# A grouped convolution on TensorE cut into four 32-row pieces, and the start of the program put into another order

## The reference

```python
def _L0_cond_ref(x, c, weight, c_weight, bias):      # grouped convolution, N, C, L = 32, 32, 512
    out = lax.conv_general_dilated(x, weight, window_strides=(1,), padding=[(4, 4)],
                                   dimension_numbers=('NCH', 'OIH', 'NCH'), feature_group_count=4)   # 9 taps
    return out + einsum('nd,od->no', c, c_weight)[:, :, None] + bias[None, :, None]
...
    q, k, v = x @ Wq.T, x @ Wk.T, x @ Wv.T           # 32 query heads, 8 key heads, of 128; RMS norm of q and k
...
    x = x + attention(conv(x, cond_128, ...), Wq, Wk, Wv, Wo, ...)      # ALiBi, causal, 32 keys a sample
    x = x + ffn(cond2(x, cond_128, ...), int4 weights ...)              # cond2: an 8-expert gate of two GELU layers
```

## Time and profile before

| | |
|---|---|
| Time, median of 3 runs | 699.32 us (698.92 to 699.69) |
| Profiled execution | 699.47 us, of which the span of the trace is 697.6 us |
| PE busy | 682.2 us, 98% of the span |
| DVE, ACT, POOL busy | 551.8, 422.9, 468.1 us |
| Clock of PE, mean granted | 0.996 |

### The profile page before, as it was taken

One profiled execution on the slowest core, in us unless ns is written; L12 is line 12 of the kernel. 1 busy time (PEld: TensorE's weight loads), 2 busy tenths in 40 slices (PEclk: granted clock), 3 DMA queues, 4 the chain that ended last, 5 costly groups with the idle time before them and its releaser, 6 DMA issues.

```text
span 697.6 us, 14570 instructions
## 1 busy us (share of the span) xinstructions
PE 682.2 (98%) x5070; PEld 402.7 (58%) x5070; DVE 551.8 (79%) x834; ACT 422.9 (61%) x1269; POOL 468.1 (67%) x380
## 2 busy tenths in 40 slices
PE   9999999999999999999999999999899999999996
PEld 8766555656656566565665656656535555555554
DVE  4978878878869778787886977777666888888887
ACT  0478483844746557384474656637556777767773
POOL 0468874973876595497388659558337778878885
PEclk9999999999999999999999999999999999999999
DMA  7520364685387378357528627544100000010001
GB/s 244 191 87 2 136 153 109 151 214 101 83 189 160 100 152 215 91 131 226 112 68 224 129 89 157 125 100 85 9 1 1 0 1 1 1 46 16 1 0 61
DMA packets 92752, 69.20 MB, mean 99 GB/s; under 512 B 74752, under 2 KB 75296, under 8 KB 90528
## 3 DMA queue, kind: packets, MB, share of 16 engines
q1 hardware_dynamic: 92560, 68.34, 39.1%
q10 hardware_dynamic: 144, 0.26, 0.1%
HBM read 51.68 MB, written 2.21 MB: 77 GB/s over the span
## 4 chain that ended last, share of the span: by engine, by line
PE 83%; POOL 6%; DVE 4%; issue 4%; ACT 2%; DMA 1%; SPq 0%; DVEq 0%; POOLq 0%; ACTq 0%
PE bank L612 20%; PE bank L613 19%; PE bank L614 19%; PE bank L972 3%; PE bank L973 3%; PE bank L941 3%; PE bank L942 3%; PE bank L664 2%; PE bank L959 2%; PE bank L960 2%; POOL wqlo L1984 2%; PE bank L801 1%; PE bank L759 1%; PE bank L786 1%; PE bank L774 1%
## 5 line engine op out<-in xcount | busy, mean ns | idle before, releaser
L612 PE MATMUL bank<-wohi,oThi 128*128 128x512 f16 x256 | 97.1, 379 | 2.2 <-DVE oTlo L1666 2.1
L612 PE MATMUL bank<-wqhi,cThi 128*128 128x512 f16 x256 | 97.0, 379 | 0.8 <-POOL wqlo L1984 0.6
L613 PE MATMUL bank<-wolo,oThi 128*128 128x512 f16 x256 | 97.0, 379 | 0.0
L614 PE MATMUL bank<-wohi,oTlo 128*128 128x512 f16 x256 | 97.0, 379 | 0.0
L614 PE MATMUL bank<-wqhi,cTlo 128*128 128x512 f16 x256 | 97.0, 379 | 0.0
L613 PE MATMUL bank<-wqlo,cThi 128*128 128x512 f16 x256 | 97.0, 379 | 0.0
L1129 ACT ACTIVATE qraw<-bank 128x512 f32<-128x512 f32 x64 | 37.8, 591 | 78.4 <-PE bank L614 77.6
L1674 DVE SCALAR_TENSOR_TENSOR x<-bank,ysc,x 128x512 f32<-128x512 f32 x64 | 47.8, 748 | 45.0 <-PE bank L614 44.8
L2032 POOL TENSOR_TENSOR qinv<-qms,neghalf 128x8 f32<-128x8 f32 x28 | 52.6, 1879 | 39.0 <-ACT qms L1148 39.0
L1140 ACT ACTIVATE qsq<-qraw 128x128 f32<-128x128 f32 x256 | 75.4, 299 | 1.7
L1994 POOL TENSOR_TENSOR wolo<-wor,wohi 128x512 f16<-128x512 f32 x32 | 40.3, 1278 | 49.6 <-ACT wohi L1109 49.6
(11 more groups left out here) (217 smaller groups left out, 1853.8 us busy)
## 6 DMA issues: line engine op xcount, KB each, us to landing
wqr<-in_wq SPq DMA_DIRECT2D x8, 1024.0 KB, 7.4
wor<-in_wo SPq DMA_DIRECT2D x8, 1024.0 KB, 6.0
raw<-in_gu_w SPq DMA_DIRECT2D x28, 256.0 KB, 3.1
zeros<-in_gu_z SPq DMA_DIRECT2D x28, 256.0 KB, 4.5
wkvr<-in_wkv SPq DMA_DIRECT2D x8, 512.0 KB, 7.2
srow<-in_up_s SPq DMA_DIRECT2D x14, 256.0 KB, 5.2
raw<-in_dn_w SPq DMA_DIRECT2D x14, 256.0 KB, 2.7
zeros<-in_dn_z SPq DMA_DIRECT2D x14, 256.0 KB, 3.7
```

Source lines behind the costliest of these rows:

```text
L612: mm(o, ahi, bhi, start=start and k == 0, stop=False)
L613: mm(o, ahi, blo, start=False, stop=False)
L614: last = mm(o, alo, bhi, start=False, stop=stop and k == n - 1)
```

## The change

Each 128-row matmul of the convolution becomes four of 32 rows, one for each channel group: group `g` has its channels and phases in partitions 32g to 32g + 31 (the host lays `xT` and `cwr` out so), its moving weights are 32 by 32 with no zeros, and it writes its own bank: `bank[4 * half + g]` for all four quads of a half. `cwf`, `mask` and their load are gone. So `conv_out` is called for a half and a group, after the half's last quad; and the maximum over `cf` is one reduction over a half.

The first query weights aren't scaled in place: ACT writes `wqhi` from `wqr` with the scale, DVE writes `wqlo` with it. Unit 0's `wqlo` no longer runs on POOL.

The order changes: the gate's whole chain stands between quads 3 and 4; quads 6 and 7 behind the first projection; `maxima_rows(2)` and `maxima_all(2)` later, between the last key and value tiles; the table load for Exp and the Exp before `conv_high(0)` on ACT; the reductions over `wqr`, `wkvr` and `cf` behind all of half 0's `conv_out` and the gate on DVE.

```diff
-            def conv(q, samples=range(BQ)):
+            def conv(q):
+                half, t = divmod(q, HQ)
                 pe.wait_ge(arrived[q], 16)
-                if q >= 2:
-                    pe.wait_ge(d_cf, q - 1)
-                out4 = PA[q % 2][:, :].rearrange("p (c b s) -> p c b s", c=PH, b=BQ)
-                for b in samples:
+                if q == 0:
+                    pe.wait_ge(l_conv, 16)
+                elif q == HQ:
+                    pe.wait_ge(d_ctxb, 2)
+                    pe.wait_ge(d_lg, 1)
+                for b in range(BQ):
                     for j in range(SHIFTS):
-                        last = mm(out4[:, :, b, :], xT[:, BQ * q + b, j:j + P], cwf[:, j, :, :, :],
-                                  start=j == 0, stop=j == SHIFTS - 1)
-                if b == BQ - 1:
-                    last.then_inc(t_conv, 1)
+                        for g in range(NGRP):
+                            rows = slice(PH * CG * g, PH * CG * g + PH * CG)
+                            out4 = bank[HQ * half + g][:, :].rearrange("p (c t b o) -> p c t b o", c=PH, t=HQ, b=BQ)
+                            last = mm(out4[:, :, t, b, :], xT[rows, BQ * q + b, j:j + P], cwr[rows, j, :, :],
+                                      start=j == 0, stop=j == SHIFTS - 1)
+                            if t == HQ - 1 and b == BQ - 1 and j == SHIFTS - 1:
+                                last.then_inc(t_conv, 1)
 
             pe.wait_ge(d_ones, 1)
             for _ in range(8):
                 mm(PC[3][:, 0:P], ones[:, :], ones[:, :], start=True, stop=True)
-            pe.wait_ge(d_cwf, 1)
             conv(0)
+            conv(1)
             context()
-            conv(1)
             conv(2)
+            conv(3)
             gate_layer1()
-            conv(3)
             gate_layer2()
+            gate_logits()
+            gate_spread()
             conv(4)
-            gate_logits()
-            conv(5, range(1))
+            conv(5)
             maxima_rows(1)
-            conv(5, range(1, 3))
             maxima_all(1)
-            conv(5, range(3, BQ))
-            conv(6)
-            gate_spread()
-            conv(7)
 
 
             def project_q(u, half, kv, t):
...
                 if half == 0 and t == 0 and not (isinstance(u, int) and u == 0):
-                    pe.wait_ge(p_wq, KC * kv + KC)
+                    pe.wait_ge(p_wq, KC * kv)
...
-                if not half:
-                    pe.wait_ge(d_cf, NQ - 1 if t == 0 else NQ)
                 project_q(u, half, 0, t)
 
             first_project_q(0, 0, 0)
+            conv(6)
+            conv(7)
             first_project_q(0, 0, 1)
             first_project_q(0, 0, 2)
+            first_project_q(0, 0, 3)
+            project_kv(0, 0, 0, (0,))
             maxima_rows(2)
-            first_project_q(0, 0, 3)
+            project_kv(0, 0, 0, (1,), (2,))
             maxima_all(2)
-            project_kv(0, 0, 0)
+            project_kv(0, 0, 0, (1,), (3,))
...
+            act.wait_ge(d_lg, 1)
+            A(le[:, :, :], lg[:, :, :], ACT.Exp).then_inc(a_lexp, 1)
             conv_high(0)
+            for c in range(KC):
+                A(wqhi[:, c, :], wqr[:, c, :], ACT.Copy, scale=wup[:, M_Q:M_Q + 1]).then_inc(a_wq, 1)
             conv_high(1)
-            split_wq(0)
             conv_high(2)
...
-            dve.wait_ge(l_conv, 32)
-            V.tensor_tensor(cwf[:, :, :, :, :].rearrange("p j f g o -> p (j f) g o"),
-                            cwr[:, :, :, None, :].rearrange("p j f a o -> p (j f) a o").broadcast_to(
-                                [P, SHIFTS * PH, NGRP, CG]),
-                            mask[:, None, :, None].broadcast_to([P, SHIFTS * PH, NGRP, CG]),
...
-            def conv_out(q):
-
-                dve.wait_ge(t_conv, q + 1)
+            def conv_out(h, g):
+
+                dve.wait_ge(t_conv, HQ * h + g + 1)
                 dve.wait_ge(d_ctxb, 2)
-                V.tensor_tensor(cf[:, q, :, :, :].rearrange("p c b s -> p c (b s)"),
-                                PA[q % 2][:, :].rearrange("p (c n) -> p c n", c=PH),
-                                ctxb[:, None, BQ * q:BQ * q + BQ, :].rearrange("p a b s -> p a (b s)").broadcast_to(
-                                    [P, PH, P]), ALU.add).then_inc(d_cf, 1)
+                V.tensor_tensor(cf[:, h, :, :, CG * g:CG * g + CG],
+                                bank[HQ * h + g][:, :].rearrange("p (c n o) -> p c n o", c=PH, n=HB),
+                                ctxb[:, None, HB * h:HB * h + HB, CG * g:CG * g + CG].broadcast_to([P, PH, HB, CG]),
+                                ALU.add).then_inc(d_cf, 1)
 
             def conv_low(q):
                 dve.wait_ge(a_cThi, q + 1)
-                V.scalar_tensor_tensor(cTlo[:, q, :, :], cf[:, q, :, :, :].rearrange("p c b s -> p c (b s)"),
+                V.scalar_tensor_tensor(cTlo[:, q, :, :], conv_tile(q),
                                        cup[:, q // HQ:q // HQ + 1], cThi[:, q, :, :], ALU.mult,
                                        ALU.subtract).then_inc(d_cTlo, 1)
 
-            def conv_max(q):
-                dve.wait_ge(d_cf, q + 1)
-                link(V.tensor_reduce(cmax[:, q:q + 1], cf[:, q, :, :, :].rearrange("p c b s -> p (c b s)"), AX_X,
-                                     ALU.max, apply_absolute_value=True))
-
             def conv_maximum(h, col):
-                return V.tensor_reduce(mx[:, col:col + 1], cmax[:, HQ * h:HQ * h + HQ], AX_X, ALU.max)
+                dve.wait_ge(d_cf, HQ * h + HQ)
+                return V.tensor_reduce(mx[:, col:col + 1], cf[:, h, :, :, :].rearrange("p c b s -> p (c b s)"), AX_X,
+                                       ALU.max, apply_absolute_value=True)
+
+            def first_wq_low():
+                for c in range(KC):
+                    dve.wait_ge(a_wq, c + 1)
+                    V.scalar_tensor_tensor(wqlo[:, c, :], wqr[:, c, :], wup[:, M_Q:M_Q + 1], wqhi[:, c, :], ALU.mult,
+                                           ALU.subtract).then_inc(d_wqlo, 1)
...
-            conv_max(0)
-            conv_out(1)
+            for g in range(NGRP):
+                conv_out(0, g)
+            gate_rows()
+            gate_logits()
             link(weight_max(M_Q, wqr, l_wq, 0))
-            conv_out(2)
-            conv_max(1)
             link(weight_max(M_KV, wkvr, l_wkv, 0))
-            conv_out(3)
-            conv_max(2)
-            conv_max(3)
             conv_maximum(0, M_O).then_inc(d_mx, 1)
-            conv_out(4)
             dve.wait_ge(l_const, 16)
             maxima_diagonal(1)
             maxima_powers(1)
             conv_scale(0, M_O)
+            conv_low(0)
+            first_wq_low()
+            conv_low(1)
             norm_eps(0, 1)
-            scale_wq()
-            gate_rows()
-            conv_out(5)
-            conv_low(0)
+            conv_low(2)
...
             scale_wkv()
-            conv_low(1)
-            conv_out(6)
-            gate_logits()
-            dve.wait_ge(t_mx, 1)
-            link(weight_max(M_O, wor, l_wo, 0))
-            conv_out(7)
-            conv_low(2)
+            conv_low(3)
...
-            conv_low(3)
-            for q in range(HQ, NQ):
-                conv_max(q)
+            for g in range(NGRP):
+                conv_out(1, g)
+            link(weight_max(M_O, wor, l_wo, 0))
             conv_maximum(1, M_C).then_inc(d_mx, 1)
```

More of the change, by code:

```diff
@@ L152, in build @@
         cwr = sb("cwr", [P, SHIFTS, PH, CG], F32, early)
-        cwf = sb("cwf", [P, SHIFTS, PH, NGRP, CG], F32, early)
-        mask = sb("mask", [P, NGRP], F32, early)
         fs = sb("fs", [P, S], F32, early)
@@ L160, in build @@
         ctxb = sb("ctxb", [P, B, S], F32, early)
-        cf = sb("cf", [P, NQ, PH, BQ, S], F32, early)
+        cf = sb("cf", [P, 2, PH, HB, S], F32, early)
         w0 = sb("w0", [P, P], F32, early)
@@ L293, in build @@
         d_wn = sem("d_wn")
-        d_cwf = sem("d_cwf")
+        d_wqlo = sem("d_wqlo")
         d_cTlo = sem("d_cTlo")
@@ L425, in chain, with conv_tile @@
             return link
-        def quads(u_half):
-            return range(HQ * u_half, HQ * u_half + HQ)
+        def conv_tile(q):
+            first = BQ * (q % HQ)
+            return cf[:, q // HQ, :, first:first + BQ, :].rearrange("p c b s -> p c (b s)")
         side = PC[2]
@@ L495, in _ @@
         def _(sp):
-            sp.dma_start(mask[:, :], mask_in).then_inc(l_conv, 16)
             sp.dma_start(cwr[:, :, :, :], conv_in).then_inc(l_conv, 16)
@@ L524, in load_wq @@
             def load_wq(kv):
-                sp.wait_ge(p_wq, KC * kv)
+                if isinstance(kv, int) and kv == 1:
+                    sp.wait_ge(d_wqlo, KC)
+                else:
+                    sp.wait_ge(p_wq, KC * kv - KC)
                 sp.dma_start(wqr[:, :, :], wq_in[kv]).then_inc(l_wq, 16)
@@ L1086, in conv_high @@
                 act.wait_ge(d_cup, q // HQ + 1)
```

(13 more changed lines are left out.)

12 lines of the change are left out of this document (3 added, 9 removed).

## The result

The changed kernel takes 732.49 us (median of 4 runs, 726.66 to 735.31), the kernel before 699.2 us beside it: a ratio of 1.0462, 95% interval 1.0429 to 1.0496. The forecast was 731.6 us. The figure stands, but the reason given for most of it does not: the four row groups overlap completely, and what costs is TensorE's clock.

The account below looks back on a forecast made before the run. PE, at 98% of the span, was taken to bound the kernel. Terms 21.3 + 4.5 + 0 + 3.5 + 2.0 + 0.5 + 1.5 - 1.0 = 32.3 us on a median of 699.32 gave 731.6 us; range 706 to 740, 80%.

Parts of the forecast that it names:

- Row groups: Convolution: each group's second pass holds up the next group for one weight load, 0.444 us a sample and shift, +21.3 us.
- A: Rival for the convolution: row groups overlap fully, 0.222 us a sample and shift, no change there; 711 us in all, 28%.
- The price of a weight load: Convolution: an f32 load of 128 columns costs 0.11 us whatever moves behind it; 32 rows don't make it cheaper.
- The clock: PE's clock falls to its lower level at the gate's gap, perhaps twice: nothing to 3 us, taken as +1.5.
- case C: Rival: no overlap of f32 loads, or queued groups with the clock low throughout; about 773 us, 12%.
- B: The prediction's own case for the convolution: groups queue in line, 0.444 us a sample and shift; 731.6 us, 44%.
- Gate: Gate's four matmuls in one piece before quad 4: 5.4 us in which PE works about 0.9, +4.5 us.
- First maxima: DVE's reductions behind the gate, 5.8 us, are covered by quads 4 and 5: 0 us.
- First projection: Wait for `cThi`, `cTlo` and DVE's first `wqlo` piece before L607: 4.1 us less the 0.63 of before, +3.5.
- Second maxima: `maxima_all(2)` has one key and value tile behind it where it had four: 0 to 3.6 us, taken as +2.0.
- Tile changes: Switches between 32-row and full matmuls on PE, some four more blocks of this kind: +0.5 us.
- Given back: Later PE idle time absorbs some of the loss, at most the 1.4 us of 60 to 81 us: -1.0 us.

Follow-up runs that it names:

- wide tiles: Changed kernel with 128 moving columns instead of 32 in each 32-row convolution matmul, so other values: 716.46 us, ratio 1.0252 to the kernel before.
- best order: Changed kernel with 128-row matmuls, gate spread between quads, quads 6 and 7 ahead of the first projection, later second maxima kept in part: 700.30 us, ratio 1.0019.
- order alone: Changed kernel's order, splits and host layout, but 128-row convolution matmuls over `cwf` as before and a bank for each quad: 713.05 us, ratio 1.0207.
- the first profile: Profiled run of the changed kernel in its first comparison with the kernel before: 735.3 us, where the median was 732.49 us.
- the second: Profiled run of the unaltered changed kernel, measured once more against the kernel before: 727.36 us, where the median was 729.38 us.
- gate and cover: Changed kernel, 32-row tiles kept, with the gate's pieces between quads again and quads 6 and 7 round `maxima_all(1)`: 723.33 us, ratio 1.0328.
- more dummies: Changed kernel with 20 instead of 8 matmuls over `ones` ahead of the convolution: 727.68 us, ratio 1.0420.
- repaired gate: Changed kernel's order with 128-row matmuls and the gate's pieces put between quads again: 709.84 us, ratio 1.0151.

## Why the prediction was right and wrong

**Row groups: wrong.** The step that failed is "matmuls of other groups wait in line behind one that waits for its weights", read from the earlier trace rows. It priced 96 x 0.222 us of extra time at full clock; the passes show 0.222 us in all, and wide tiles cost what 128 rows do. The rows themselves spoke against it: L653 holds row group 0, whose matmul is the first of the four in the program, so a queue behind it would make all four late, and only one was. The same trace gives the four loads (min/median/max ns):

```profile
L801 PEld LDWEIGHTS bank<-pThi,vhi x4: 90/91/140, 67.7 to 67.8; 32*128 32x128 f16 x4
```

The load of 140 ns is the first of the four, row group 0's, behind L653's in the same group. If the late matmul is that group's own, the other three passed it, and the earlier trace rows are a case of A; the trace doesn't name a matmul's group, so this is a reading and not shown. I had one observation of a different mix and made it the rule. The rule of the Trainium skill that stood beside it ("TensorE: Matmul & The Clock Gate", Part 3, "The mechanism") was taken to mean the same. The trace agrees with its part on loads, which overlap matmuls of other row groups; on the order of starts it can't decide, as records name neither row group nor pass. No group waits there for another's load. The earlier trace rows were the right analogue.

**The price of a weight load: right.** 32 rows don't make it cheaper and moving columns don't matter: at full clock a pass was 0.111 or 0.112 us with 128, 64 and 32 columns, in tiles or not.

**The clock: wrong by the size of the forecast.** The term was 1.5 us. By 0.44 us for each microsecond at the lower level, the profiled run's 63.6 us less before's 1.5 cost 27 us (23 by 0.37). The mechanism stood in the text, in case C ("because 32-row passes with few columns leave PE looking idle"), but on top of B and with 12%; the reason given against it, that the first block's passes got faster while they ran, was about passes of 128 columns, which the change removes. The case that happened, A's overlap with C's clock, was not among the cases. That its time equals B's is chance: at the lower clock 0.222 us becomes 0.43, and B said 0.444. So the forecast of 731.6 us was met by luck: a term of 21.3 us that isn't there stood in for one of 23 to 27 us that was put at 1.5.

**The order.** *Gate:* 4.5 forecast, 1.72 + 0.38 + 0.47 + 0.92 = 3.5 idle. The last sentence of the prediction allowed for shorter handovers: `gate_logits` on DVE took 0.74 us where it had taken 1.68, its last instruction 0.22 instead of 1.20. Why is open; a less loaded DVE isn't it alone, as the best order has 0.22 there too. *First maxima:* 0, right. *First projection:* 3.5 forecast, 0.79 + 3.21 less the 0.6 of before = 3.4. *Second maxima:* 2.0 forecast, 3.0. *Tile changes:* 0.5 forecast, none seen: the next line starts 5.57 us after the first two quads' start with wide tiles, 5.54 with 128 rows. *Given back:* not seen to be more than 1. The order alone cost 13.9 us (13.1 in the profiled run) with 9.9 of idle time and 8.7 us more at the lower level, 3.8 by the price above: 13.7.

**The sum.** For the first profile 9.9 + 27 = 37, measured 735.3 - 699.47 = 35.8; for the second 9.9 + 19 = 29, measured 27.9. The same sum (699.47 + waits + 0.44 for each us at the lower level) misses the wide tiles, the order alone, the gate and cover kernels by 1.1 us at most, the ones with 32 and 64 columns in 128 rows by 2.2 and 2.6, and the one with more dummies, with its 3.9 us of later start and the 1.9 us wait, by 4.3 (732.2 for 727.84; 1.2 of it because the time at the lower level ahead of the tiles is in the later start too). It leaves out the 3.4 us at the lower level that some of the traces, before's too, show once past 500 us. Idle time at the lower level costs nothing and isn't the same share everywhere, so this is what such a rule can give.

**Open.** What about few moving columns goes with the lower level isn't settled: runs with 128, 64 and 32 columns were made, and nothing else of the passes varied. Convolution tiles with correct values and 128 moving columns (three quarters zeros) were not tried; by the wide tiles they would cost what 128 rows do and gain nothing.

## What to carry to other kernels

Before cutting a matmul into row tiles, ask what sets the time of a pass: here neither the rows nor the moving columns do, and the f32 load of 128 stationary columns is what is left (fewer stationary columns weren't tried). Tiling in rows leaves it as it is, so four overlapping tiles only equal the one full matmul, zeros and all. Read the clock of every block of the new form, not PE's busy share: leaving out useless columns cost 15.8 us in 128-row matmuls with the same loads, and 16 to 19 us in tiles. And where a block of matmuls covers a chain of handovers on other engines, keep it cut in pieces between them; put in one piece, each handover was paid in full (10.5 us here), and the clock fell behind two of them, for 10.2 us in the order alone.

## What the hardware showed beyond that

- Four f32 matmuls of 32 rows, one for each row group, of two passes each overlap fully: 8 loads and 8 matmuls in 0.222 us at full clock, starts within a pass 7 ns apart.
- With passes of 32 moving columns the granted clock fell to 0.50 in stretches in which PE was busy for 100%, in two different kernels (tiles and none); with 128 columns it fell in the first 100 us only behind waits of 3 us or more in all (the gate's 3.5, the first projection's 4.0, the second maxima's 3.0), and not behind the 0.9 us of the repaired gate.
- With 64 columns it held until a gap, and did not come back in the 10.5 us of such passes behind it; behind the first projection, whose last matmuls ran at full clock, two quads of such passes ran at full clock for 5.3 us.
- In one of the tile kernels PE stood for 1.88 us behind 183 passes at full clock with nothing in the profile that released it; 192 such passes later in the same trace had no such wait.
